# A recommendation scorer on one core: seven tiles to a TensorE loop, rows copied earlier, 75-column histogram matmuls

## What is computed

```python
item_emb = concatenate([table_i1[item[:, 0]], table_i2[item[:, 1]], table_i3[item[:, 2]]], axis=1)
ub = concatenate([table_i1[rec_his[:, :, 0]], table_i2[rec_his[:, :, 1]], table_i3[rec_his[:, :, 2]]], axis=2)
mask = rec_his[:, :, 0] == 0
q = broadcast_to(item_emb[:, None, :], ub.shape)
att_in = concatenate([q, ub, q - ub, q * ub], axis=-1)
score = ((att_in @ w_att1.T + b_att1) @ w_att2.T + b_att2)[..., 0]
score = where(mask, 0.0, score)
browse = einsum('bl,ble->be', score, ub)
x = dice(concatenate([item_emb, browse, user_emb], -1) @ w1.T + b1)   # two layers with batch statistics
x = dice(x @ w2.T + b2)
return sigmoid(x @ w3.T + b3)[:, 0]
```

## Time and profile before

| | us |
|---|---|
| median of 3 runs | 1789.54 |
| lowest, highest | 1787.26, 1792.01 |
| the profiled execution, own time | 1791.8 |
| its span, first to last instruction | 1790.0 |
| mean granted TensorE clock | 0.946 |

### The profile page before, as it was taken

The page is one execution under the profiler, slowest core; times in us unless marked ns, Lnnn a source line. Parts: engine busy times, 40 slices in busy tenths (PEclk is TensorE's granted clock), DMA queues, the critical chain, the costliest instruction groups (busy, mean ns, idle before and its releaser), DMA issues. The chain is left out here.

```text
span 1790.0 us, 76739 instructions
## 1 busy us (share of the span) xinstructions
PE 1531.2 (86%) x31007; PEld 1410.1 (79%) x31007; DVE 1462.4 (82%) x1514; ACT 1177.5 (66%) x1921; POOL 1272.0 (71%) x1988
## 2 busy tenths in 40 slices
PE   5798989899897988989799798988979798898975
PEld 4788878788787888878788787888878788887862
DVE  6699887979787797888879788797888789889964
ACT  5576766667575676766567576676756567675546
POOL 3588677877776786777777777787777677767850
PEclk8799999999898999999899899999999899899986
DMA  2111020211102011120201102011110201102000
GB/s 35 50 50 52 25 75 19 72 28 43 49 25 67 23 50 43 28 73 16 76 23 47 46 25 67 26 49 41 46 56 16 77 22 50 43 24 73 22 21 0
DMA packets 33047, 74.85 MB, mean 42 GB/s; under 512 B 15471, under 2 KB 20463, under 8 KB 28911
## 3 DMA queue, kind: packets, MB, share of 16 engines
q1 hardware_dynamic: 25656, 68.48, 13.2%
q0 software_dynamic: 2144, 1.36, 0.8%
q10 hardware_dynamic: 4952, 0.28, 0.2%
HBM read 7.02 MB, written 0.01 MB: 4 GB/s over the span
## 5 line engine op out<-in xcount | busy, mean ns | idle before, releaser
L755 ACT ACTIVATE hiT<-hiT_ps 128x800 bf16<-128x800 bf16 x512 | 429.6, 839 | 352.2 <-PE hiT_ps L514 346.4
L550 PE MATMUL wsum_ps<-scaled_lo,onehot_hi 100*128 100x78 bf16 x12288 | 553.0, 201 | 60.3 <-DVE scaled_lo L986 56.7
L974 DVE TENSOR_REDUCE score_j<-sel 100x24 f32<-100x600 f32 x512 | 397.4, 776 | 253.0 <-PE sel L536 251.3
L536 PE MATMUL sel<-scoretab,hiT 128*128 128x75 bf16 x12288 | 540.3, 202 | 69.7 <-DMA scoretab<-scores_b 63.6
L536 PEld LDWEIGHTS sel<-scoretab,hiT 128*128 128x128 bf16 x12288 | 501.6, 100 | 122.9 <-issue 86.2
L550 PEld LDWEIGHTS wsum_ps<-scaled_lo,onehot_hi 100*128 100x128 bf16 x12288 | 509.2, 100 | 75.7 <-DVE scaled_lo L986 65.8
L986 DVE TENSOR_TENSOR scaled_lo<-onehot_lo,parts 100x3744 bf16<-100x3744 bf16 x256 | 546.3, 2134 | 19.3 <-POOL parts L424 15.0
L763 ACT ACTIVATE wsum_ring<-wsum_ps 128x300 f32<-128x300 f32 x512 | 359.9, 703 | 185.2 <-PE wsum_ps L550 151.1
L410 POOL TENSOR_TENSOR score<-score_j 100x16 f32<-100x16 f32 x256 | 236.4, 923 | 329.0 <-DVE score_j L974 325.7
L514 PE MATMUL hiT_ps<-identb,onehot_hi 100*128 100x100 bf16 x4096 | 274.0, 211 | 88.5 <-issue 76.2
L413 POOL TENSOR_TENSOR score<-score,score_j 100x16 f32<-100x16 f32 x256 | 318.5, 1244 | 20.1
(11 more groups left out here) (158 smaller groups left out, 1017.6 us busy)
## 6 DMA issues: line engine op xcount, KB each, us to landing
scoretab<-scores_b SPq DMA_DIRECT2D x96, 375.0 KB
weightsum<-wsum_ring SPq DMA_DIRECT2D x128, 125.0 KB
weightsum<-wsum_ring SPq DMA_DIRECT2D x64, 150.0 KB
raw<-in_r_rec_his_dram SPq DMA_DIRECT2D x32, 150.0 KB, 2.6
item_rows<-in_L_rec_table_i_dram,ids_now POOLq DMA_INDIRECT x51
table_blk<-in_L_rec_table_i_dram SPq DMA_DIRECT2D x3, 125.0 KB
user_rows<-in_L_rec_table_user_dram,ids_now POOLq DMA_INDIRECT x16, 4.1
weightsum<-in_L_rec_w_dram ACTq DMA_DIRECT2D x6, 25.0 KB
```

The source lines that it names most:

```text
L536: mm = pe.matmul(o, rows, scoretab[0:HJ, s // 16, :, b, i, :], start=(i == 0), stop=(i == 2))
L550: mm = pe.matmul(wsum_ps[:, b * U:(b + 1) * U], hi_columns(n % 4, g), scaled_lo[:, n % 2, g, i % 3, :], start=(i == 0), stop=(i == 5))
L755: act.activation(hiT[:, s % 2, 0:8 * POS], hiT_ps[:, 0:8 * POS], ACT.Copy).then_inc(hiT_copied, 1)
L974: dve.tensor_reduce(score_j[:, n % 2, g0:g0 + 8, :].rearrange("p (q c) j -> p q (c j)", q=2), sel[0:POS, 2 * (s % 2):2 * (s % 2) + 2, 0:4 ...
```

## The change

There are three edits. PE's middle tiles are written out seven to a pass, so that its loop runs 2 passes over the same 14 tiles; the other engines keep their loops. ACT's `lo_rows` moves from the end of an even slot to right behind `copy_hiT`. The sums' matmuls take 25 of the 26 columns of each feature as moving operand and write 75 columns, and `copy_sums` copies them as they lie.

```diff
@@
+        RUN = 7
+        assert (TILES - 2) % RUN == 0
@@ add_scores
-                        mm = pe.matmul(wsum_ps[:, b * U:(b + 1) * U], hi_columns(n % 4, g),
-                                       scaled_lo[:, n % 2, g, i % 3, :], start=(i == 0), stop=(i == 5))
+                        mm = pe.matmul(wsum_ps[:, b * W:(b + 1) * W].rearrange("p (j v) -> p j v", j=NF), hi_columns(n % 4, g),
+                                       scaled_lo[:, n % 2, g, i % 3, :].rearrange("p (j v) -> p j v", j=NF)[:, :, 0:LO],
+                                       start=(i == 0), stop=(i == 5))
@@ PE, the tiles
-            with pe.Fori(1, TILES - 1) as t:
-                for s in range(SLOTS):
-                    slot(t, s)
+            with pe.Fori(0, (TILES - 2) // RUN) as run:
+                for i in range(RUN):
+                    for s in range(SLOTS):
+                        slot(run * RUN + (i + 1), s)
@@ copy_sums
                 act.activation(wsum_ring[:, (s // 8) % 2, :, 4 * (s % 8):4 * (s % 8) + 4]
-                               .rearrange("p (j l) b -> p b j l", j=NF),
-                               wsum_ps[:, 0:4 * U].rearrange("p (b j l) -> p b j l", b=4, j=NF)[:, :, :, 0:LO], ACT.Copy
+                               .rearrange("p u b -> p b u"),
+                               wsum_ps[:, 0:4 * W].rearrange("p (b u) -> p b u", b=4), ACT.Copy
@@ ACT, slot
                     copy_hiT(t, s + 1)
                 elif not last:
                     copy_hiT(t + 1, 0)
+                if s % 2 == 0 and s < SLOTS - 2:
+                    lo_rows(t, s // 2 + 1)
+                elif s % 2 == 0 and not last:
+                    lo_rows(t + 1, 0)
                 here = tasks_of(t)
@@ ACT, end of slot
                     split_copy(i // 3, i % 3, 3 * NR * (t + 1) + i + 1)
-                if s % 2 == 0 and s < SLOTS - 2:
-                    lo_rows(t, s // 2 + 1)
-                elif s % 2 == 0 and not last:
-                    lo_rows(t + 1, 0)
```

## The result

| | before | after |
|---|---|---|
| median | 1790.78 | 1650.89 |
| lowest to highest of 4 runs | 1787.26 to 1795.70 | 1650.01 to 1651.48 |
| profiled execution, own time | 1791.8 | 1650.01 |
| its span | 1790.0 | 1648.2 |
| granted clock | 0.946 | 0.960 |

The ratio is 0.922, 95% interval 0.919 to 0.924: 139.9 us less, where the sum of the prediction was 139. That the total fits doesn't show that its terms do.

A forecast was written before the change was run, and what follows sets the result against it. Waits, not a full engine, make the time: PE's bound in slots 1 to 21, DVE's in 22 to 31. Jumps 67 plus stalls and columns 67, tile 0 4, tile 15 1, make 139 us less: forecast 1650, range 1616 to 1692.

The forecast's parts named there:

- Part 1: PE's loop, seven tiles to a pass: 12 jumps back fewer at 5.6 us each, 67 us less.
- Part 2: `lo_rows` behind `copy_hiT`: PE's stalls before transposes in slots 1 to 21 go, 4.45 us per tile; slots 22 to 31 nothing.
- DVE's floors: Steps of two slots can't fall below DVE's 5.3 to 5.5 us; steps 0, 2, 7, 8, 9 lose 1.55 us.
- ACT's 0.4 us in slots 20 and 21: ACT also copies digits there, 6.2 us of work against PE's 5.8, so 0.4 us of gain stays away.
- POOL's 0.3 per tile: Cost of POOL's gathers and two `make_keep` in shorter steps: 0.3 us per tile, bounds zero and 2.7.
- Part 3: Sums' matmuls with 75 columns: 0.025 us per slot, 0.3 us per tile in the 12 PE-bound slots.
- The slower rival: Sums' matmuls reading runs of 25 elements at half rate: about 1900 us, deciding from 11 ns each; chance 0.02.
- The signs: Right: tiles about 96 us, one long wait before reads. Wrong: tiles outside 94 to 98.5, or sums' matmuls longer than reads'.
- The boundary stays: At tile ends, the named DMA or another engine's jump keeps the 67 us: 1717; chance 0.07.
- POOL or ACT: POOL or ACT becomes the bound; POOL's chain doesn't fit beside gathers, 2.7 us per tile: 1688; chance 0.18.
- more gain: POOL and ACT absorb everything and DVE-bound slots gain too, 6.5 us per tile instead of 4.75: 1625; chance 0.12.
- No effect: The change doesn't bite, both waits having other causes: 1790; chance 0.02.

The follow-up runs named there:

- p2_lorows: Kernel of before with only `lo_rows` moved behind `copy_hiT`: 1712.15 us, ratio 0.953.
- lo_mid: Kernel of after with `lo_rows` between `copy_sums` and `split_copy` instead of right behind `copy_hiT`: 1661.95 us, ratio 0.928 to before.
- p1_unroll: Kernel of before with only PE's tiles 1 to 14 written out seven to a pass: 1725.51 us, ratio 0.962.
- dve_light: Kernel of after with DVE's `onehot_low` done only in the first two steps: 1604.92 us, ratio 0.895 to before.
- p3_cols: Kernel of before with only the sums' 75-column matmuls and the plainer copy: 1789.90 us, ratio 0.998.
- no_gather: Kernel of after without POOL's gathers of items and users behind the first tiles: 1647.02 us, ratio 0.919 to before.
- before_nohalf1: Kernel of before without the transfers of the second half of `scoretab` behind tile 0: 1774.63 us, one execution.
- full_unroll: Kernel of after with all 14 middle tiles of PE written out, no loop on PE: 1644.01 us, ratio 0.918 to before.
- cols75c: Kernel of after with the first 75 of the 78 columns as one run in the sums' matmuls: 1640.62 us, one execution.

## Why the prediction was right, and where not

**The views.** Its three readings hold, with the slot of the first one misnumbered (9, not 8), which changes no number: "issue" was `lo_rows` (p2_lorows, lo_mid), the DMA before the reads was the jump (p1_unroll), and the last slots are DVE's (dve_light).

**Part 1, right.** 67 us for twelve jumps; alone they gave 65.4. The 5.6 us for one is a mean over branches between 3.3 and 6.6 us (4.8), plus restart. The prediction took it from totals of 13 tiles, and that was right, though tile 14, its measure of a tile without a jump, flattered it: 101.0 us had been worked out, and p1_unroll's tiles without a jump take 101.4 on average; from the earlier trace rows alone, a short one, it would have come out at some 4 us. The register operations cost nothing that shows. Of the Trainium skill's two rules, the 108 ns that Advanced Engine Details and Errata, Control Flow Timing, gives for a compare-and-branch would have meant 1716 by the prediction's estimate; the trace shows 0.08 us where PE's branch is not taken, and 3.3 to 6.6 us where it is. The rule of Runtime: NRT & Kernel Launch, Instruction fetch mechanics, that a far target must be fetched, agrees with the two instruction packets per jump.

**Part 2, the mechanism right, the inside of the sum partly wrong.** Slots 1 to 21 of tile 14 took 69.57 us and take 64.59: 4.98, where 5.15 - 0.4 - 0.3 + 0.3 = 4.75 had been said. Behind it:
- DVE's floors take about the share of the gain that was said, but in other steps. Step 2 (slots 4 and 5) fell from 5.56 to 4.89, below the 5.3 that was called its floor, and step 3, whose gain was counted as kept, fell only from 6.96 to 6.82, since slot 6 took some back (3.06 to 3.49). Steps 7 and 8 gained 0.64 and 0.44, and step 9 nothing (5.61 to 5.71). So PE met its waits for DVE a step or two later than the forecast put them.
- ACT's 0.4 us in slots 20 and 21 don't stand there: 6.76 fell to 5.77. They stand in slot 22, which grew by 0.29 us: ACT works through without a pause, its copies of `hiT` 6.18 us apart, as read from the earlier trace rows (6.2), and PE waits 0.20 us for its copy of the sums.

```profile
1460.55 0.84 ACT L759 ACTIVATE hiT<-hiT_ps 128x800 bf16<-128x800 bf16 x1
...
1466.73 0.90 ACT L759 ACTIVATE hiT<-hiT_ps 128x800 bf16<-128x800 bf16 x1
```

- POOL's 0.3 per tile, chosen by judgement between 0 and 2.7, isn't in the tiles: without the gathers their slots take as long as with them. Zero, the lower bound, was right.
- Slots 22 to 31 were put at nothing. They take 28.25 us in tile 14 of before and 28.3 to 29.7 in after. The edit of `lo_rows` isn't the cause: p1_unroll, without it, takes 28.4 to 29.5 there. The two tiles of after that are as short as tile 14 of before (3 and 10; 28.3 and 28.4) are those in whose end the granted clock doesn't fall (last section).
- Tile 0 gave 1.4 us, not 4. Its stalls went, but its steps have no "finish" and lie near DVE's 5.3 to 5.5 already, so that an even slot took back what an odd one gained: steps 5, 8 and 9 took 5.56, 5.68 and 5.62 us before and take 5.55, 5.70 and 5.72. Tile 15 and the layers gave 2.1, with 1 expected.

**Part 3, wrong.** 0.3 us per tile, 4 us in all, was said; p3_cols gives 1.0 with an interval that takes in zero, its slots gained nothing, and slots 8 of before and after are equal (3.33). The step that failed is "so the new form should cost what it costs", where "it" is L536. The 12.7 us between two groups of the page held other differences than three columns: in after, with 75 columns in both, the two groups still differ by 17.0 us. And of the columns' own effect the runs of 25 took back what was saved. The slower rival, 11 ns more per matmul, is also out: the runs cost some 2 ns per matmul.

**The sum.** Tiles 1 to 14 gave 134.2 us against 133.5 forecast. In them the trace of p1_unroll gives 64.2 to the jumps, where 67 had been said, and leaves 70.0 to the rest, where 66.5 had been said: both terms are right in kind, and that their misses cancel is luck. Tile 0 gave 2.6 less than forecast, tile 15 and the layers 1.1 more, and 4.1 us came from ahead of tile 0, where the change does nothing: that is a difference of the two profiled executions. Without it the span would have been 1652.3, and the forecast of 1651 1.3 us too low. The total is nearer than the terms deserve.

**The signs.** Those for "right" came true, with tiles 7 and 8, at the jump that is left, outside the 96 us. One sign for "wrong" came true as well: a matmul of the sums takes longer than one of the reads, 38 ns against 35 from start to start. It did so before the change too, so it could not tell the outcomes apart.

**Rivals.** *The boundary stays*: refuted by p1_unroll. *POOL or ACT* (1688): refuted by the result, and its cause by no_gather; *more gain* (1625) by the result, and dve_light shows the floor in the last slots that it denied. *No effect* and *slower* by the result.

## What to carry to other kernels

An engine whose loop body is thousands of instructions pays for each jump back in microseconds, and the profile shows it as a wait for whatever was last to arrive: compare the loop's boundary with one in straight code, then write the body out, for that engine alone. Look at what stands ahead of a small operation in the program of an in-order engine when another engine waits for it; moving 0.34 us of work three places forward was worth as much as twelve jumps. Behind both, find the floor of the next engine step by step before a gain is added up; work that is moved out of a step in which PE already waits for DVE is given back in the next.

## What the runs showed of the hardware

**A jump's price depends on transfers.** With three transfers of `scoretab` under way seven of PE's branches in before took 3.3 to 3.8 us and six 5.8 to 6.6; without them all 13 took 3.4 to 3.8 (before_nohalf1). The one jump of after took 4.1, that of p1_unroll 3.8. PE's loop body has some 1900 matmuls. The other engines' jumps, with bodies of about a hundred such instructions, take 0.2 to 0.3 us to the next instruction.

**The granted clock also falls without a long gap.** In tile 14 of after, PE waits 1.32 and 1.96 us for `scaled_lo` in slots 28 and 30, with full slots between, and runs at the lower level behind it. PE's rows, then windows of one microsecond (busy of PE, PEld, DVE, ACT, POOL, then PEclk):

```profile
1483.23 1.06 PE L552 MATMUL wsum_ps<-scaled_lo,onehot_hi 100*128 100x75 bf16 x24 [1.32 <-DVE scaled_lo L990]
...
1489.76 1.52 PE L552 MATMUL wsum_ps<-scaled_lo,onehot_hi 100*128 100x75 bf16 x24 [1.96 <-DVE scaled_lo L990]
1491.09 1.72 PE L538 MATMUL sel<-scoretab,hiT 128*128 128x75 bf16 x24
```

```profile
1489.00:1490.00 1.00, 0.24 (x7) 0.24 (x8) 1.00 (x2) 0.00 (x0) 1.00 (x2) 1.00 0.00 0
...
1491.00:1492.00 1.00, 1.00 (x20) 1.00 (x18) 1.00 (x2) 0.68 (x1) 0.92 (x3) 0.50 0.08 16
```

It happens in most tiles; in tiles 3 and 10, where it doesn't, slot 31 takes 2.5 to 2.6 us instead of 3.1 to 3.6, and the tile 95.5 instead of 96.1 to 96.6 (tiles 7 and 8, at the jump, left out). Tile 10 has the same two waits, 1.32 and 1.96 us, so they alone don't decide it. With DVE relieved (dve_light) it has gone from the ends of the tiles, and the mean clock is 0.972.

**The start has two modes, 3 to 4 us apart.** Tile 0's first read starts at 46.3 to 46.9 us in the profiled executions of six kernels (after, p3_cols, full_unroll, lo_mid, no_gather, cols75c) and at 49.5 to 50.7 in the other eight, though no edit is at work there. In all eight the clock was granted at half for 6.8 us, from 20.0 to 22.4 us on, and in none of the six. Before, then after:

```profile
24.00:25.00 1.00, 1.00 (x7) 1.00 (x6) 1.00 (x1) 0.00 (x0) 0.70 (x2) 0.50 0.12 16
```

```profile
24.00:25.00 1.00, 1.00 (x11) 1.00 (x11) 1.00 (x1) 0.87 (x2) 0.70 (x2) 1.00 0.13 23
```

What decides between them stays open. A difference of 4 us or less between two of these kernels should be read from the tiles, not from the totals. Even there it can be the clock at the tiles' ends or the length of a jump, as in no_gather.
